# Reordered weight loads, a GpSimd subtraction and direct constants in the table stage of a fused transformer block on one core

## The reference

```python
q_exp = jnp.where(row_zero[..., None], 0.0, q[:, None, :])
self_feat = jnp.concatenate([exp_v, q_exp], axis=-1) @ W_self.T + b_self
output = self_feat
for d in range(2):
    A = (adj_f if d == 0 else jnp.swapaxes(adj_f, 1, 2))[:, :, :20, :]
    cond, vb = A.sum(-1), A @ w_bias + b_bias
    kv = self_feat[:, :20]
    qh = (self_feat @ Wq[d].T + bq[d]).reshape(B, N, 16, 32)
    kh = (kv @ Wk[d].T + bk[d]).reshape(B, 20, 16, 32)
    aff = jnp.einsum('bnhd,bmhd->bnhm', qh, kh) / np.sqrt(32)
    aff = jnp.where(cond[:, :, None, :] > 0, aff, NEG) + vb[:, :, None, :]
    w = jax.nn.softmax(aff, axis=-1)
    out_t = jnp.einsum('bnhm,bmf->bnhf', w, kv)
    output += jnp.einsum('bnhf,hgf->bnhg', out_t, Wout[d]).reshape(B, N, 512) + bout[d]
x = exp_v + jax.nn.relu(output)
```

## Time and profile before

| | us |
|---|---|
| median of 3 runs | 2922.01 (2920.53 to 2923.34) |
| profiled execution | 2919.6 |
| its span | 2917.8 |
| PE busy | 2843.4 (97%) |
| DVE busy | 2216.7 (76%) |
| ACT busy | 1602.1 (55%) |
| POOL busy | 1050.4 (36%) |

### The profile page before, as it was taken

One profiled execution on the slowest core, in us unless ns is written; L12 is line 12 of the kernel. 1 busy time (PEld: TensorE's weight loads), 2 busy tenths in 40 slices (PEclk: granted clock), 3 DMA queues, 4 the chain that ended last, 5 costly groups with the idle time before them and its releaser, 6 DMA issues. The chain is left out here.

```text
span 2917.8 us, 68187 instructions
## 1 busy us (share of the span) xinstructions
PE 2843.4 (97%) x27746; PEld 2435.0 (83%) x27746; DVE 2216.7 (76%) x2955; ACT 1602.1 (55%) x3253; POOL 1050.4 (36%) x675
## 2 busy tenths in 40 slices
PE   8898999999999999999999999999999999989998
PEld 6788889999887777777777777777788999989998
DVE  4699986555536888888888888888577766687876
ACT  2566653332214777777777777777233565554442
POOL 1222110000001444444444444446556555573332
PEclk9999999999999999999999999999999999999999
DMA  7222236553695433333333333332564555587775
GB/s 240 79 99 67 95 128 225 213 217 102 217 317 152 117 88 88 89 88 90 94 89 92 92 89 88 89 96 88 188 245 141 206 203 198 218 291 227 242 241 173
DMA packets 277104, 445.06 MB, mean 153 GB/s; under 512 B 37848, under 2 KB 152696, under 8 KB 273224
## 3 DMA queue, kind: packets, MB, share of 16 engines
q1 hardware_dynamic: 267940, 434.48, 45.8%
q0 software_dynamic: 576, 6.29, 0.5%
q10 hardware_dynamic: 8292, 0.05, 0.2%
HBM read 266.99 MB, written 173.74 MB: 151 GB/s over the span
## 5 line engine op out<-in xcount | busy, mean ns | idle before, releaser
L1889 DVE TENSOR_REDUCE head_nm<-b_ps 128x1 f32<-128x1024 f32 x510 | 599.2, 1216 | 16.3 <-PE b_ps L1832 3.3
L1800 ACT ACTIVATE b_p<-b_ps,head_nm 128x1024 f32<-128x1024 f32 x510 | 562.2, 1112 | 0.0
L1861 PE MATMUL b_po<-b_pt,b_v 128*64 128x256 f32 x4096 | 498.4, 385 | 0.8 <-DVE b_pt L1909 0.8
L1805 ACT ACTIVATE b_pt<-b_tp_act 128x512 f32<-128x512 f32 x512 | 307.8, 601 | 307.9 <-PE b_tp_dve L1844 307.9
L1909 DVE COPY b_pt<-b_tp_dve 128x512 f32<-128x512 f32 x512 | 350.9, 686 | 116.6 <-PE b_tp_dve L1844 116.6
L1844 PEld LDWEIGHTS b_tp_act<-ident,b_p 64*128 64x128 f32 x4096 | 311.3, 138 | 125.0 <-issue 100.4
L1861 PEld LDWEIGHTS b_po<-b_pt,b_v 128*64 128x64 f32 x4096 | 271.9, 136 | 128.6 <-ACT b_pt L1805 0.9
L1844 PE MATMUL b_tp_act<-ident,b_p 64*128 64x64 f32 x4096 | 347.3, 225 | 2.4 <-issue 2.4
L1844 PE MATMUL b_tp_dve<-ident,b_p 64*128 64x64 f32 x4096 | 347.8, 225 | 0.0
L1844 PEld LDWEIGHTS b_tp_dve<-ident,b_p 64*128 64x128 f32 x4096 | 311.5, 138 | 9.1
L2389 POOL TENSOR_TENSOR d_blocks<-d_blocks 128x512 f32<-128x512 f32 x124 | 181.8, 1466 | 112.2 <-ACT d_blocks L2441 105.6
(11 more groups left out here) (444 smaller groups left out, 7605.7 us busy)
## 6 DMA issues: line engine op xcount, KB each, us to landing
b_raw_q<-q_t SPq DMA_DIRECT2D x124, 256.0 KB, 4.3
x_mlp_raw<-hidden_blocks SPq DMA_DIRECT2D x112, 256.0 KB, 3.7
d_x_second_raw<-hidden_blocks SPq DMA_DIRECT2D x112, 256.0 KB, 3.4
hidden_blocks<-d_blocks SPq DMA_DIRECT2D x32, 768.0 KB, 3.5
k_t<-p_out SPq DMA_DIRECT2D x64, 256.0 KB, 2.2
q_t<-p_out SPq DMA_DIRECT2D x64, 256.0 KB, 2.3
v_n<-p_out SPq DMA_DIRECT2D x64, 256.0 KB, 3.5
b_v<-v_n SPq DMA_DIRECT2D x32, 512.0 KB, 3.9
```

The source lines that it names most:

```text
L1800: act.activation(pr[k % 4][:], ps[k % 2][:], ACT.Exp, bias=nm[:, k % 4:k % 4 + 1], accum_out=rs[:, n:n + 1]).then_inc(exp_done, 1)
L1805: act.activation(dst, src, ACT.Copy).then_inc(t_out[0], 1)
L1861: mm = pe.matmul(po[rows, (blk % 2) * 2 * P:(blk % 2 + 1) * 2 * P], vt[u][:, kc, rows], pt[blk % 2][h][:, kc, :], start=(kc == 0), stop=(k ...
L1889: dve.tensor_reduce(nm[:, k % 4:k % 4 + 1], ps[k % 2][:], axis=AX.X, op=ALU.max, negate=True).then_inc(max_done, 1)
```

## The change

Wq is loaded as two DMAs, one per direction, and PE waits for each half before its transposes. The untransposed W_self is loaded ahead of Wout. GpSimd, no longer VectorE, subtracts to make `ws_rest`, behind its first fills. The product with Wout stands behind the second of the eight large products (`PN_AT = 1`), in banks 2 and 3, and the modulations move to behind products 2 to 5. Within each large product the pass that needs `ws_rest` is now the last. GpSimd waits for Wout's landing, no longer for W_self's, before it issues W_mod.

For batch 0 the four bias rows of self_feat are loaded into `c4` early, and the high and rest constants go from `cgh` and `cgl` straight into `c4`, SBUF to SBUF, in sixteen DMAs. They stand ahead of the eight writes to `cg`. `table_rows` is cut in two, and only its part for the values (`value_rows`) runs for batch 0.

```diff
-    MOD_AT = {0: 1, 3: 2, 5: 3}
+    MOD_AT = {2: 0, 3: 1, 4: 2, 5: 3}
+    PN_AT = 1
-        PN_BANK = (4, 6)
+        PN_BANK = (2, 3)
@@ SP
-            sp.dma_start(wq[:], t["wq"].rearrange("d (k p) n -> p d k n", p=P)).then_inc(wq_in, 16)
+            for d in range(2):
+                sp.dma_start(wq[:, d], t["wq"][d].rearrange("(k p) n -> p k n", p=P)).then_inc(wq_in[d], 16)
             sp.dma_start(ws_t[:, 0:KC, :], ws_parts[:, 0:KC, :]).then_inc(ws_x_in, 16)
             sp.dma_start(wk[:], t["wk_t"].rearrange("d (k p) n -> p d k n", p=P)).then_inc(wk_in, 16)
+            sp.dma_start(ws_n[:, :, 0:F], t["ws"].rearrange("(k p) n -> p k n", p=P)[:, :, 0:F]).then_inc(ws_n_in, 16)
             sp.dma_start(wo[:], t["wo_t"].rearrange("d (k p) n -> p d k n", p=P)).then_inc(wo_in, 16)
-            sp.dma_start(ws_n[:, :, 0:F], t["ws"].rearrange("(k p) n -> p k n", p=P)[:, :, 0:F]).then_inc(ws_n_in, 16)
...
-            sp.wait_ge(cg_written, 4)
+            sp.wait_ge(first.zeros, 6)
+            sp.wait_ge(css_out, 32)
+            for part in range(2):
+                for r, row in enumerate((0, B)):
+                    sp.dma_start(first.c4[2 * part + r:2 * part + r + 1, 0:F].bitcast(F32), cg[part, row:row + 1, B * A0:]
+                                 ).then_inc(first.tab_in[0], 16)
+            cut = A0 // NT
+            for part, src in enumerate((cgh, cgl)):
+                sp.wait_ge(cg_written, 3 + part)
+                for r, row in enumerate((0, B)):
+                    for n in range(NT):
+                        sp.dma_start(first.c4[2 * part + r:2 * part + r + 1, F + n * cut:F + (n + 1) * cut].bitcast(F32),
+                                     src[n * TW + row:n * TW + row + 1, slot_of(0) * cut:(slot_of(0) + 1) * cut].bitcast(F32)
+                                     ).then_inc(first.tab_in[0], 16)
             for part, src in enumerate((cgh, cgl)):
                 for n in range(NT):
                     sp.dma_start(cg[part, :, 0:B * A0]...
-            sp.wait_ge(first.zeros, 6)
-            sp.wait_ge(css_out, 32)
             sp.wait_ge(out_done, OUT_ALL)
-            table_rows(sp, 0, first.c4, first.bd, cg, pn, first.tab_in[0], out_done)
+            value_rows(sp, 0, first.bd, pn, out_done)
@@ GpSimd
-            pool.wait_ge(ws_n_in, 16)
+            pool.wait_ge(ws_split, 1)
+            pool.tensor_tensor(ws_rest[:], ws_n[:], ws_high[:], ALU.subtract).then_inc(ws_split, 1)
+            pool.wait_ge(wo_in, 16)
@@ PE
-            pe.wait_ge(wq_in, 16)
             for j in range(2 * KC):
+                if j % KC == 0:
+                    pe.wait_ge(wq_in[j // KC], 16)
...
-            pe.wait_ge(wo_in, 16)
-            for d in range(2):
-                ... product with Wout ...
-            modulation(0)
-            pe.wait_ge(ws_split, 2)
             for j in range(2 * KC):
-                if j < 2:
-                    pe.wait_ge(pn_copied, j + 1)
-                    pe.wait_ge(q8_done, 2)
-                else:
+                if j == 0:
+                    pe.wait_ge(ws_split, 1)
+                if j >= 2:
                     pe.wait_ge(m1_copied, j - 1)
-                for m, (w_, s_) in enumerate(((wqt_l, ws_high), (wqt_h, ws_rest), (wqt_h, ws_high))):
+                for m, (w_, s_) in enumerate(((wqt_l, ws_high), (wqt_h, ws_high), (wqt_h, ws_rest))):
+                    if j == 0 and m == 2:
+                        pe.wait_ge(ws_split, 2)
...
+                if j == PN_AT:
+                    pe.wait_ge(wo_in, 16)
+                    pe.wait_ge(kb_written, 8 * KC)
+                    ... product with Wout ...
@@ VectorE
-            dve.wait_ge(ws_split, 1)
-            dve.tensor_tensor(ws_rest[:], ws_n[:], ws_high[:], ALU.subtract).then_inc(ws_split, 1)
```

More of the change, by code:

```diff
@@ L179, in table_rows, with value_rows @@
             queue.dma_start(dst[:, F:], cg[part, row:row + 1, slot_of(b) * A0:(slot_of(b) + 1) * A0]).then_inc(tab_in, 16)
+    value_rows(queue, b, bd, pn, bd_in)
+def value_rows(queue, b, bd, pn, bd_in):
     for c in range(NC0):
@@ L265, in graph_tables @@
             "act_out dve_out gh_done gl_done")
[L266 to L269, removed]
+        (b_mod_in, silu_done, mod_done, mod_t_done, mod_rows_done, mod_rows_t, gates_done, gates_copied) = sems(
+            chain, nc, "tables", "b_mod_in silu_done mod_done mod_t_done mod_rows_done mod_rows_t gates_done gates_copied")
+        ws_in, ws_x_in, ws_n_in, wk_in, wo_in, css_out, out_done, gates_out = sems(
+            chain, nc, "tables", "ws_in ws_x_in ws_n_in wk_in wo_in css_out out_done gates_out")
+        wq_in = sems(chain, nc, "tables", "wq_in0 wq_in1")
         w_mod_in = [nc.alloc_semaphore("tables_w_mod_in%d" % i) for i in range(2)]
@@ L385, in _ @@
         def _(pool):
-            pool.memset(ident[:], 0.0).then_inc(id_ready, 1)
-            pool.wait_ge(id_ready, 1)
+            pool.memset(ident[:], 0.0).then_inc(pool_done, 1)
+            pool.wait_ge(pool_done, 1)
             pool.affine_select(out=ident[:], in_=ident[:], compare_op=ALU.not_equal, fill=1.0, base=0,
-                               pattern=[[-1, P]], channel_multiplier=1).then_inc(id_ready, 1)
+                               pattern=[[-1, P]], channel_multiplier=1).then_inc(pool_done, 1)
             pool.memset(silu_t[:], 0.0).then_inc(pool_done, 1)
@@ L448, in _ @@
             mm.then_inc(q_done, 1)
-            pe.wait_ge(id_ready, 2)
+            pe.wait_ge(pool_done, 2)
             pe.wait_ge(dve_step, 4)
@@ L486, in _ @@
                 mm.then_inc(kh_done, 1)
-            pe.wait_ge(wo_in, 16)
-            for d in range(2):
-                for k in range(KC):
-                    mm = pe.matmul(ps[PN_BANK[d]][0:R0, :], sf_t[:, k, :], wo[:, d, k, :], start=(k == 0), stop=(k == KC - 1))
-                mm.then_inc(pn_done, 1)
-            modulation(0)
-            pe.wait_ge(ws_split, 2)
             for j in range(2 * KC):
-                if j < 2:
-                    pe.wait_ge(pn_copied, j + 1)
-                    pe.wait_ge(q8_done, 2)
-                else:
+                if j == 0:
+                    pe.wait_ge(ws_split, 1)
+                if j >= 2:
                     pe.wait_ge(m1_copied, j - 1)
-                for m, (w_, s_) in enumerate(((wqt_l, ws_high), (wqt_h, ws_rest), (wqt_h, ws_high))):
+                for m, (w_, s_) in enumerate(((wqt_l, ws_high), (wqt_h, ws_high), (wqt_h, ws_rest))):
+                    if j == 0 and m == 2:
+                        pe.wait_ge(ws_split, 2)
                     for k in range(KC):
@@ L505, in _ @@
                 mm.then_inc(m1_done, 1)
+                if j == PN_AT:
+                    pe.wait_ge(wo_in, 16)
+                    pe.wait_ge(kb_written, 8 * KC)
+                    for d in range(2):
+                        for k in range(KC):
+                            mm = pe.matmul(ps[PN_BANK[d]][0:R0, :], sf_t[:, k, :], wo[:, d, k, :], start=(k == 0), stop=(k == KC - 1))
+                        mm.then_inc(pn_done, 1)
                 if j in MOD_AT:
@@ L509, in _ @@
                     pe.wait_ge(first.rs_done, 1)
+                    pe.wait_ge(pn_copied, 2)
                     for c in range(KC):
@@ L568, in _ @@
             dve.wait_ge(q_done, 2)
-            dve.wait_ge(pool_done, 3)
+            dve.wait_ge(pool_done, 5)
             dve.tensor_copy(q8[:, :, 0:B], ps[7][:, 0:KC * TW].rearrange("p (k b) -> p k b", b=TW)[:, :, 0:B])
@@ L575, in _ @@
             dve.tensor_copy(wsh[:], ws_t[:, 0:KC, :]).then_inc(ws_done, 1)
-            dve.wait_ge(pool_done, 5)
+            dve.wait_ge(pool_done, 7)
             for dc in range(2 * KC):
@@ L627, in _ @@
                     ALU.add).then_inc(mod_t_done, 1)
-            dve.wait_ge(pool_done, 6)
+            dve.wait_ge(pool_done, 8)
             dve.wait_ge(m1_copied, 2 * KC)
@@ L928, in logits @@
                 if k % BT == 0:
-                    pe.wait_ge(tab_in[b % 2], TAB * (b // 2 + 1) - (0 if b % 2 else BD))
+                    pe.wait_ge(tab_in[b % 2], TAB * (b // 2 + 1) + (0 if b % 2 else 16 * (4 + 16) - TAB))
                 if k == 0:
```

4 lines of the change are left out of this document (2 added, 2 removed).

## The result

| | before | after |
|---|---|---|
| median of 10 runs, us | 2922.86 (2920.53 to 2925.15) | 2930.36 (2925.38 to 2932.66) |
| ratio, 95% interval | | 1.0024 (1.0014 to 1.0033) |
| profiled execution, its span | 2919.6, 2917.8 | 2932.4, 2930.6 |
| mean granted clock | 0.994 | 0.991 |

The change makes the kernel 7.5 us slower, which is clear of no difference: 0.14 to 0.33%. The forecast was 2920.8, no change, with 3% for slower.

The account below looks back on a forecast made before the run. PE is 97% busy, so only the start can move, with first tiles hanging on SP's queue too. Gain 1.9 less 0.75 gives -1.15: 2919.6 becomes 2918.4, plus 2.4 is 2920.8 us; range 2916.8 to 2924.4.

Parts of the forecast that it names:

- 3% for slower: Chance of a median above 2927.9 us, by the GpSimd rival with bad luck or two mishaps together.
- Wq in halves: Table stage start: half the transposes run before Wq's second half lands; gain 1.1 us, bounds 0 and 1.85.
- W_self and GpSimd: After the K product: W_self lands at 28.0, GpSimd's rest takes 5.1 us; PE's 1.17 us stall goes.
- The rival in which GpSimd holds VectorE: Table stage: GpSimd's subtraction shuts out VectorE's K copies for 5.1 us, time 2926.0; 8%.
- W_mod: Modulations: third load takes 7.4 us and stalls PE 0.4, bounds 0 and 2.4; late-landing rival 2922.9, 15%.
- the front's 1.9: PE leaves the tables 1.9 us earlier: 1.1 from Wq, 1.2 from W_self, less 0.4 for W_mod.
- Constants: Tables to graph stage: PE starts 1.4 us earlier, but SP's queue delays the third x tile; tile 1 0.75 later.
- Sixteen are 4.7 (5.9 by the other row): SP time for the sixteen constant copies: 4.7 us at 0.29 each, or 5.9 at 0.37, from HBM rows.
- the two small terms of the queue: SP's queue behind the constants: cg's writes and their wait 4.1 us, then twenty value rows 7.35.
- PE's own gap: PE's idle before the first graph product shrinks from 2.85 to about 1.4 us.
- The rival that the earlier start carries through: Graph start: third x tile does not hold ScalarE, VectorE follows PE; 5.0 us gained, 2917.0; 7%.
- a bound of 2.0: Upper bound on the 0.75 us cost of tile 1's delay from the sixteen copies, at 0.37 us per row.

Follow-up runs that it names:

- b4: Kernel before with only the Wq load cut in two halves, one run: 2922.98 us.
- c2: b4 again, with 11 runs (kernel before, only Wq in halves): 2924.01 us, ratio 1.0005.
- a2: Kernel before with only the sixteen direct SBUF-to-SBUF constant copies ahead of cg's writes: 2933.71 us, ratio 1.0034.
- c3: Kernel before with only a4's graph start (four direct copies, value rows behind the x loads of tiles 2 and 3): 2920.41 us, ratio 0.9991.
- c1: a1 again, with 11 runs (changed front, constants by HBM as before): 2921.44 us, ratio 0.9997.
- a1: Changed kernel with batch 0's constants written to cg and loaded from HBM as before; the front stays: 2924.73 us, ratio 1.0001.
- b2: Changed kernel with its sixteen SBUF-to-SBUF copies cut into 4 pieces of 160 bytes each: 2926.45 us, ratio 1.0014.
- b3: Changed kernel with constants from HBM in eight rows and value rows behind the x loads of tiles 2 and 3: 2922.07 us, ratio 0.9997.
- c4: a4 again, with 11 runs (changed front together with c3's graph start): 2918.84 us, ratio 0.9986.
- a3: Changed kernel with the sixteen SBUF-to-SBUF copies made four strided DMAs of four pieces: 2922.46 us, ratio 0.9995.
- a4: a3 with the twenty value rows moved behind the x loads of tiles 2 and 3: 2919.50 us, ratio 0.9988.
- b1: Changed front, cg written first, constants loaded from HBM in sixteen pieces of 160 numbers instead of four rows: 2925.67 us, ratio 1.0006.

## Why the prediction was wrong

**Wq in halves: right for the profile that it was read from.** Forecast 1.1, measured, from the end of the first product, 1.04 in b4 and 1.03 in c2 (19.21 less 13.22 is 5.99, for 7.03 before). But in a2 and c3, with Wq whole, the same distance was 5.93 and 6.13: behind a first product of 5.9 or 6.0 us the halves win next to nothing. The forecast took the 5.04 of its one profile as given. By themselves the halves won no time. In b4 and c2 the first tile's products ran longer, too; this window of c2 (PE, PEld, DVE, ACT, POOL busy, PEclk, DMA share, GB/s) answers to the second of the earlier trace rows:

```profile
87.60:94.40 6.80, 6.78 (x29) 6.77 (x30) 0.00 (x0) 0.00 (x0) 1.89 (x7) 0.57 0.08 11
```

The granted clock there is 0.57, against 0.71, and from the first product to tile 0's softmax it took 6.82 us for 5.75, which is the gain. Why it falls further in these two than in c1 (0.71) or a1 (0.73) stays open.

**W_self and GpSimd: right, with one term too small and one too large.** W_self landed at 29.13, 1.1 later than the 28.0 of the forecast, and ScalarE's cast ended at 31.1. The subtraction took 4.58 us, where I had taken 5.1 by proportion; the Trainium skill's "GPSIMD Engine Reference", section on elementwise cycle accounting, gave an estimated 4.6, and the trace agrees with the page. The stall was 0 as forecast. In a1 the rest was ready at 30.78 + 4.61 = 35.39 and wanted at 36.06, a cover of 0.7 for the 1.0 forecast; in the profile after, where the product started 1.7 later, it was 2.0. The rival in which GpSimd holds VectorE fell: the K copies took 10.51 us beside it, 10.50 without. The Trainium skill, "SBUF — State Buffer", section "Who interferes with whom", says that a VectorE instruction with at most one SBUF input, outside the modes that take the shared ports, doesn't contend with GpSimd. For these copies the trace agrees.

**W_mod: right in size, with one load overlooked.** In the profile after, the third load, issued at 53.24, landed after 7.0 us, at 60.24, and modulation 2 started without a wait. I had charged 0.4, at 7.4.

```profile
53.24 0.53 POOL L420 DMA_DIRECT2D g_w_mod<-w_mod  x1 [16.29 <-PE g_ps L446]
...
60.42 1.50 PE L446 MATMUL g_ps<-g_w_mod,g_silu_t 128*32 128x512 f32 x16
```

The fourth load, which the forecast doesn't count, made PE wait in six of the nine profiles with this front, 0.27 us (b2) to 0.89 (c1); in b3 PE waited 0.33 for the third.

**So the front's 1.9 is the gain of a1,** whose last table part ends at 84.80 for 86.77, and it is 1.0 in the mean. In the profile of the change it is 0.65, behind a first product of 6.51 us.

**Constants: the step that failed is "Sixteen are 4.7 (5.9 by the other row)".** The sixteen took 12.0. Both of my rows were loads from HBM; the change copies between SBUF partitions, which no row of before shows, and I took the bound from rows of the other kind. The rest of the step holds nearly as it stands with this one number put in. On the axis of before (0.65 added to the profile's times) the third x tile was to be issued at 95.6 and came at 103.66, 8.1 later: 7.3 by the sixteen (12.0 for 4.7), 0.2 by the writes and their wait (4.3 for 4.1), 0.6 by the value rows (7.98 for 7.35). Tile 1 was to start at 102.24 + 0.75 = 103.0, and came at 111.1, 8.1 later. The mechanism (the gap before PE's first product doesn't decide, SP's queue up to the third x tile does) was the right one. The forecast with the measured 12.0 in it would have been 2920.8 + 7.3 = 2928.1, and with the two small terms of the queue 2928.9. The front's 1.0 for 1.9, and a median of before that is 2922.9 over ten runs for 2922.0 over three, make it 2930.7, for a measured 2930.4. PE's own gap, which I let shrink from 2.85 to 1.4 us, grew to 6.78.

**The rival that the earlier start carries through** had 7% because SP would have to be quick. c3 and c4 are that rival, made true: with four copies and x first, PE starts 0.10 us behind the last table part, the granted clock stays at 1.00, and tile 1 is 2.9 us nearer. The window of c4 that answers to the second of the earlier trace rows:

```profile
85.10:89.40 4.30, 4.22 (x30) 4.25 (x31) 1.20 (x3) 0.00 (x0) 2.10 (x7) 1.00 0.03 8
```

From the first product to the softmax of tile 0 it took 93.99 - 88.24 = 5.75 us at 0.71 and 89.36 - 85.18 = 4.18 here at 1.00, 1.57 us less, where the prediction had put 1.7 on it.

**The chances.** 3% for slower rested on a bound of 2.0 for a term that had no row. The writes to `pn` took 12.16 / 8 = 1.5 us each, and nothing said that the new copies are nearer to the loads than to these. With that row as the far end, slower would have deserved a chance many times as large. It would have been no true price either: the same eight writes took 4.78 us in the changed kernel and 3.52 in a1, so the 12.16 hangs on when they are issued; by what is not shown.

## What to carry to other kernels

Count DMA issues on the queue that issues them, and price each by rows of its own kind of source and target and its number of pieces; a copy that saves a trip through HBM can cost more of the queue than the trip. When a queue feeds two consumers, put first what the engine without slack waits for (x), and last what has slack (the values). A wait removed shows only when the next wait behind it is taken away too: here constants and x gave 0.5 and 0.2 us alone and 2.9 together. And before counting the gain of a wait in front of an engine, see how much the time of the work ahead of the wait differs between executions: the wait may have been taking the difference up, as the one for Wq did.

## What the runs showed of the hardware

- Time on SP from issue to issue: a row from HBM, 0.285 to 0.29 us; SBUF to SBUF in four pieces, 0.51 to 0.59, for pieces of 160 and of 640 bytes alike; SBUF to SBUF as one row that goes in 16 pieces of 40 bytes, 0.63, but for two of each sixteen: 1.15 and 1.89 us long in the changed kernel, 1.45 and 1.58 in a2, so 0.75 in the mean.
- The first product of the kernel, the same eight instructions in every kernel, took from 5.03 (a1) to 6.51 us (after). Its weight loads in the timelines, the last three of a1 and the last two of the changed kernel:

```profile
10.95 0.09 PEld L456 LDWEIGHTS g_ps<-g_ws_t,g_c_t 128*4 128x4 f32 x1 [0.51 <-issue]
11.38 0.09 PEld L456 LDWEIGHTS g_ps<-g_ws_t,g_c_t 128*4 128x4 f32 x1 [0.34 <-issue]
11.80 0.09 PEld L456 LDWEIGHTS g_ps<-g_ws_t,g_c_t 128*4 128x4 f32 x1 [0.34 <-issue]
```

```profile
12.21 0.13 PEld L467 LDWEIGHTS g_ps<-g_ws_t,g_c_t 128*4 128x4 f32 x1 [0.72 <-issue]
13.06 0.13 PEld L467 LDWEIGHTS g_ps<-g_ws_t,g_c_t 128*4 128x4 f32 x1 [0.73 <-issue]
```

  In a1 the step halves to 0.43 us before the end, in the other it is 0.85 to the last, while the profile's granted clock reads 1.00 over both. With Wq in halves this moves every later landmark of a profile by up to 1.5 us, so two such profiles are better compared from the end of this product. With Wq whole the wait for it takes the difference up (a2, c3), and there the comparison from that end would mislead by 0.9. The Trainium skill, "TensorE: Matmul & The Clock Gate", section on the HAM clock gate, says that the same kernel starts with another count of slow products from run to run; these traces agree, and I had not looked for it.
- TensorE idle for 1.49 us before the graph stage went on at a granted clock of 1.00 (a3, a4, c3, c4); idle for 2.7 to 2.9 us (before, a1, b3, b4, c1, c2) it ran the next 5.5 to 6.8 us at 0.57 to 0.73, and idle for 6.4 to 6.8 us (after, a2, b1) the next 6.2 to 6.9 us at 0.57 to 0.69, no lower.
